# Messages of layers 2 and 3 in two float32r parts, with half of their one-hots made on GpSimd

## The reference

```python
# layer 2
ef = jnp.concatenate([x[row], x[col], edge_attr], axis=-1)
h = ef @ W1 + b1
mu = jnp.mean(h, axis=0); var = jnp.mean((h - mu) ** 2, axis=0)
h = jax.nn.relu((h - mu) * jax.lax.rsqrt(var + BN_EPS) * gamma + beta)
msgs = h @ W2 + b2
sums = jax.ops.segment_sum(msgs, row, num_segments=n_nodes)
counts = jax.ops.segment_sum(jnp.ones((msgs.shape[0],)), row, num_segments=n_nodes)
out = sums / (counts + 1.0)[:, None] + x
# layer 3
m = jax.nn.relu(jnp.concatenate([x[src], et], axis=-1) @ msg_W.T + msg_b)
agg = jax.ops.segment_sum(m, dst, num_segments=x.shape[0])
agg = agg / jnp.clip(deg, 1.0)[:, None]
```

## Time and profile before

| | us |
|---|---|
| median of 3 runs (4504.23 to 4513.55) | 4507.58 |
| the profiled execution's own time | 4506.15 |
| its span in the trace | 4504.0 |
| layer 2, first to last h and adds of a tile | 3037 to 3812 |
| layer 3, first to last h and adds of a tile | 3884 to 4451 |

### The profile page before, as it was taken

One profiled execution on the slowest core, in us unless ns is written; L12 is line 12 of the kernel. 1 busy time (PEld: TensorE's weight loads), 2 busy tenths in 40 slices (PEclk: granted clock), 3 DMA queues, 4 the chain that ended last, 5 costly groups with the idle time before them and its releaser, 6 DMA issues.

```text
span 4504.0 us, 93109 instructions
## 1 busy us (share of the span) xinstructions
PE 3567.1 (79%) x35307; PEld 3108.5 (69%) x35307; DVE 3209.6 (71%) x7198; ACT 2176.5 (48%) x6143; POOL 964.7 (21%) x1005
## 2 busy tenths in 40 slices
PE   1488899889999451666648888669999999699996
PEld 1266666666666331666647887449999998699995
DVE  5589888878898446999868787674444445666666
ACT  2366666667777223788747667212222222333332
POOL 0466577757677400000000000000000000000000
PEclk7799998999999675878779999889999999899998
DMA  5666676767777301000011011333334432233322
GB/s 110 200 186 184 172 205 197 195 171 211 209 214 211 90 5 39 10 12 12 9 35 46 38 45 45 106 109 104 113 109 116 116 109 77 63 102 102 98 97 65
DMA packets 418314, 488.81 MB, mean 109 GB/s; under 512 B 178078, under 2 KB 329924, under 8 KB 417725
## 3 DMA queue, kind: packets, MB, share of 16 engines
q1 hardware_dynamic: 358861, 305.18, 23.7%
q0 software_dynamic: 58992, 177.50, 13.7%
HBM read 376.80 MB, written 105.72 MB: 107 GB/s over the span
## 4 chain that ended last, share of the span: by engine, by line
PE 62%; DVE 22%; ACT 5%; issue 4%; DMA 3%; SPq 2%; POOL 1%; DVEq 0%; POOLq 0%; ACTq 0%
PE bank L3533 6%; PE bank L3496 6%; PE bank L3520 5%; PE bank L3474 5%; PE bank L3476 5%; PE bank L2325 4%; PE bank L2331 3%; PE bank L2336 3%; PE bank L3442 2%; PE bank L2898 2%; PE bank L2316 2%; ACT arena_c L2861 2%; PE bank L2389 2%; PE bank L2307 2%; DVE arena_b L1749 2%
## 5 line engine op out<-in xcount | busy, mean ns | idle before, releaser
L1112 POOL DMA_INDIRECT arena_a<-src_table,src_tix x808 | 775.9, 960 | 353.1 <-issue 228.3
L3279 DVE TENSOR_SCALAR arena_c<-arena_c 128x128 f32<-128x128 f32 x1225 | 268.9, 281 | 402.4 <-PE bank L3496 402.4
L3413 ACT ACTIVATE arena_c<-bank 128x512 f32<-128x512 f32 (+2 forms) x325 | 186.5, 574 | 591.2 <-PE bank L3476 591.2
L2898 PE MATMUL bank<-arena_a,arena_c 128*128 128x150 f32 x1800 | 289.3, 331 | 173.4 <-ACT arena_c L2864 173.4
L3349 DVE TENSOR_SCALAR arena_c<-arena_c 128x128 f32<-128x128 f32 x1225 | 265.7, 280 | 203.6 <-PE bank L3533 203.6
L3474 PE MATMUL bank<-arena_c,arena_a 128*128 128x128 bf16 x3675 | 406.2, 219 | 0.0
L3476 PE MATMUL bank<-arena_c,arena_a 128*128 128x128 bf16 x3675 | 406.2, 219 | 0.0
L2898 PEld LDWEIGHTS bank<-arena_a,arena_c 128*128 128x128 f32 x1800 | 283.7, 225 | 176.5 <-ACT arena_c L2864 176.5
L3428 ACT ACTIVATE arena_c<-bank 128x512 f32<-128x512 f32 (+1 forms) x319 | 185.2, 581 | 386.8 <-PE bank L3520 386.8
L3533 PE MATMUL bank<-arena_c 128*128 128x128 f32 x2450 | 343.1, 282 | 0.0
L3496 PE MATMUL bank<-arena_c 128*128 128x129 f32 x2402 | 338.6, 281 | 0.0
(11 more groups left out here) (583 smaller groups left out, 9263.7 us busy)
## 6 DMA issues: line engine op xcount, KB each, us to landing
y_rows<-arena_c SPq DMA_DIRECT2D x101, 576.0 KB
arena_a<-bucket_rows SPq DMA_DIRECT2D x50, 832.0 KB
arena_a<-bucket_rows SPq DMA_DIRECT2D x50, 768.0 KB
arena_a<-bucket_lists SPq DMA_DIRECT2D x25, 896.0 KB, 4.6
pair_counts<-arena_c SPq DMA_DIRECT2D x25, 800.0 KB
arena_a<-bucket_lists SPq DMA_DIRECT2D x25, 704.0 KB, 4.4
arena_a<-src_table,src_tix POOLq DMA_INDIRECT x808
arena_c<-edge_attr SPq DMA_DIRECT2D x100, 128.0 KB
```

The lines of the kernel that those rows point to most:

```text
L1112: e.indirect_dma_start(out_, None, table, bass.IndirectOffsetOnAxis(ap=idx, axis=0)).then_inc(sem, 16)
L2898: put = e.matmul(bank[2 + s][:, 0:3 * KT], hot_pos[s][:, j, :], routed_v[s][:, j, :, :].rearrange("p f k -> p (f k)"), start=(j == 0), sto ...
L3279: hot = e.tensor_scalar(col_hot[at % 2][:, i, :], iota_row, src_lo[:, b, 2 * k + j:2 * k + j + 1], None, ALU.is_equal)
```

## The change

Both layers get the same edit. A message is kept as two numbers of the type float32r, a float32 of which 12 bits of the significand are kept: ScalarE's rectified message, rounded (part 0), and what the rounding left, rounded (part 1), which VectorE computes from the bank and part 0 in one instruction per group (`dve_low_parts`). The one-hots are float32r too. The adds of a tile are two float32r products of 128 columns, one per part, in place of one f32 product.

The one-hots of the first two tiles of a group stay on VectorE; those of the third and fourth go to GpSimd (`pool_b2_main`, `pool_b3`). The buffers become rings of three (`RING_M`). TensorE does the adds of group n-2 behind h of group n. A bank is free for h of group n+4 when part 1 of group n has been made, not when ScalarE has read it. The column of ones is gone; layer 2's counts come from sums that layer 1 made already (`node_sums`). The unit tests keep their place behind the one-hots of the same group. The core of the diff (the edits for layer 3 on ScalarE and TensorE are like those for layer 2):

```diff
+        RING_M = 3
+        msg_parts = part_buffers("msg_parts", base_b, 0, RING_M, [P, 2, 4, D])
+        msg_parts3 = part_buffers("msg_parts3", base_c, 7304, RING_M, [P, 2, 4, D])
+        node_hot = part_buffers("node_hot", base_a, 10752, RING_M, [P, 4, P])
...
+        def pool_b2_main(e):
+            e.wait_ge(sig.split_dve, 6)
+            for at, (u, k, bs) in enumerate(main_groups()):
+                nt = len(pair_tiles(bs))
+                if nt > 2:
+                    if at >= RING_M:
+                        e.wait_ge(sig.added_pe, at - RING_M + 1)
+                    for i in range(2, nt):
+                        hot = source_hot(e, at, i)
+                    hot.then_inc(sig.col_hot_pool, 1)
+
+        def dve_low_parts(e, at, nt, high_made, low_made, parts):
+            e.wait_ge(high_made, at + 1)
+            to = parts[at % RING_M]
+            e.scalar_tensor_tensor(out=to[:, 1, 0:nt, :], in0=bank[at % 4][:, 0:nt * P].rearrange("p (t f) -> p t f", f=P), scalar=0.0,
+                                   in1=to[:, 0, 0:nt, :], op0=ALU.max, op1=ALU.subtract).then_inc(low_made, 1)
...
                     for i, ts in enumerate(unit3_tiles(u)):
-                        if at >= 2:
-                            e.wait_ge(sig.added3_pe, at - 1)
-                        for i_, t in enumerate(ts):
-                            hot = e.tensor_scalar(col_hot[at % 2][:, i_, :], iota_row, dst_lo[:, b, t:t + 1], None, ALU.is_equal)
+                        dve_low_parts(e, at, len(ts), sig.relu3, sig.low3, msg_parts3)
+                        if at >= RING_M:
+                            e.wait_ge(sig.added3_pe, at - RING_M + 1)
+                        for i_, t in enumerate(ts[0:2]):
+                            hot = target_hot(e, at, i_, b, t)
                         hot.then_inc(sig.col_hot3, 1)
                         at += 1
                         if i == UNIT3_GROUPS[u] - 2 and u + 1 < 2 * NB:
                             dve_unit_hot3(e, u + 1)
...
-                e.activation(msgs[at % 2][:, 0:nt, 0:D], bank[at % 4][:, 0:nt * P].rearrange("p (t f) -> p t f", f=P), ACT.Relu).then_inc(sig.relu, 1)
+                e.activation(msg_parts[at % RING_M][:, 0, 0:nt, :], bank[at % 4][:, 0:nt * P].rearrange("p (t f) -> p t f", f=P), ACT.Relu).then_inc(sig.relu, 1)
...
                     if n >= 4:
-                        e.wait_ge(sig.relu, n - 3)
+                        e.wait_ge(sig.low, NB + n - 3)
...
-                if n >= 1:
-                    at = n - 1
+                if n >= 2:
+                    at = n - 2
...
                     for i in into_k:
-                        put = e.matmul(bank[6 + k % 2][:, 0:D + 1], col_hot[at % 2][:, i, :], msgs[at % 2][:, i, :],
-                                       start=(first and i == into_k[0]), stop=(last and i == into_k[-1]))
+                        for part in range(2):
+                            put = e.matmul(bank[6 + k % 2][:, 0:D], hots[:, i, :], parts[:, part, i, :],
+                                           start=(first and i == into_k[0] and part == 0), stop=(last and i == into_k[-1] and part == 1))
                     put.then_inc(sig.added_pe, 1)
```

More of the change, by code:

```diff
@@ L8 @@
 F32 = mybir.dt.float32
+F32R = mybir.dt.float32r
 I32 = mybir.dt.int32
@@ L3000, in pool_buckets, with target_hot, pool_b3 @@
             e.wait_ge(g.nodes_ready, 4)
+            pool_b2_main(e)
+            pool_b3(e)
+        def target_hot(e, at, i, b, t):
+            return e.tensor_scalar(node_hot[at % RING_M][:, i, :], iota_row, dst_lo[:, b, t:t + 1], None, ALU.is_equal)
+        def pool_b3(e):
+            e.wait_ge(sig.split_dve, 8)
+            at = 0
+            for u in range(2 * NB):
+                for ts in unit3_tiles(u):
+                    if len(ts) > 2:
+                        if at >= RING_M:
+                            e.wait_ge(sig.added3_pe, at - RING_M + 1)
+                        for i in range(2, len(ts)):
+                            hot = target_hot(e, at, i, u // 2, ts[i])
+                        hot.then_inc(sig.col_hot3_pool, 1)
+                    at += 1
         def dve_b_hot(e, b, i):
@@ L3257, in dve_b2_stats @@
             dve_wc_parts(e, own)
-            for s in range(2):
-                e.memset(msgs[s][:, :, D:D + 1], 1.0)
+            own.step(e.tensor_copy(stat[:, 2, :], node_sums[:, 0:NB, 2]))
             dve_split(e, scaled_tables, 2)
@@ L3267, in main_groups, with source_hot @@
             return [(u, u // 2, bs) for u in range(2 * NB) for bs in unit_pairs(u % 2)]
+        def source_hot(e, at, i):
+            u, k, bs = main_groups()[at]
+            b, j = pair_tiles(bs)[i]
+            return e.tensor_scalar(node_hot[at % RING_M][:, i, :], iota_row, src_lo[:, b, 2 * k + j:2 * k + j + 1], None, ALU.is_equal)
+        def pool_b2_main(e):
[13 more added lines that the diff above has]
+                                   in1=to[:, 0, 0:nt, :], op0=ALU.max, op1=ALU.subtract).then_inc(low_made, 1)
         def dve_b2_main(e, own):
             all_groups = main_groups()
-            counts = stat[:, 2, :]
             extras = 0
-            for at in range(GROUPS + 2):
+            for at in range(GROUPS + 3):
                 if at < GROUPS:
                     u, k, bs = all_groups[at]
-                    if at >= 2:
-                        e.wait_ge(sig.added_pe, at - 1)
-                    for i, (b, j) in enumerate(pair_tiles(bs)):
-                        hot = e.tensor_scalar(col_hot[at % 2][:, i, :], iota_row, src_lo[:, b, 2 * k + j:2 * k + j + 1], None, ALU.is_equal)
+                    nt = len(pair_tiles(bs))
+                    dve_low_parts(e, at, nt, sig.relu, sig.low, msg_parts)
+                    if at >= RING_M:
+                        e.wait_ge(sig.added_pe, at - RING_M + 1)
+                    for i in range(min(nt, 2)):
+                        hot = source_hot(e, at, i)
                     hot.then_inc(sig.col_hot, 1)
@@ L3353, in dve_b3 @@
                             dve_unit_hot3(e, u + 1)
[L3354 removed]
+                        if i == 3 and u % 2 == 0 and u:
                             dve_b3_block(e, b - 1)
@@ L3456, in pe_b2_main @@
             e.wait_ge(sig.d_wc, 192)
-            for n in range(GROUPS + 1):
+            by_pool = 0
+            for n in range(GROUPS + 2):
                 if n < GROUPS:
@@ L3504, in pe_b3 @@
             flat = [(u, i, ts) for u in range(2 * NB) for i, ts in enumerate(unit3_tiles(u))]
-            for n in range(len(flat) + 1):
+            by_pool = 0
+            for n in range(len(flat) + 2):
                 if n < len(flat):
@@ L3532, in pe_b3 @@
                     for i_ in range(len(ts)):
-                        put = e.matmul(bank[6 + b % 2][:, 0:D], col_hot[at % 2][:, i_, :], msgs[at % 2][:, i_, 0:D],
-                                       start=(first and i_ == 0), stop=(last and i_ == len(ts) - 1))
+                        for part in range(2):
+                            put = e.matmul(bank[6 + b % 2][:, 0:D], node_hot[at % RING_M][:, i_, :], msg_parts3[at % RING_M][:, part, i_, :],
+                                           start=(first and i_ == 0 and part == 0), stop=(last and i_ == len(ts) - 1 and part == 1))
                     put.then_inc(sig.added3_pe, 1)
```

62 lines of the change are left out of this document (38 added, 24 removed).

## The result

The changed kernel takes 4678.3 us (median of 4 runs, 4675.0 to 4687.6), against 4509.8 us for the kernel before in the same session: a ratio of 1.0382, 95% interval 1.0365 to 1.0399. It is slower, as forecast and inside the range, but by 169 us where the sum said 103. The profiled execution has a span of 4685.8 us, 182 longer than the one of before; it is the longest of the four. The ratios in this document are those on record; the quotient of two medians differs from them by up to 0.0013.

A forecast was written before the change was run, and what follows sets the result against it. TensorE's stream was taken as the bound in layers 2 and 3, the f32 weight load setting the products' pace; -35 + 78 + 29 + 10 + 20 + 1 = +103 on 4506 gave 4610 us, range 4535 to 4700.

The forecast's parts named there:

- The products: Adds on TensorE: load pace stays 0.111 us, the last pass ends sooner, 0.95 becomes 0.89; -35 us, bounds -35 and 0.
- Part 1 ahead of the unit tests: VectorE's queue: tests come late, TensorE waits 2.06 and 1.21 us at layer 3 boundaries (+78), 1.2 in layer 2 (+29).
- GpSimd and VectorE: GpSimd's one-hots and VectorE hold each other up where both run; +10 us taken, bounds nothing and 42 us.
- the 0.5 that was named: Sign to look for in the profile: GpSimd's one-hots under 0.5 us each.
- The rule of the Trainium skill: Shared port pair: VectorE instructions in a two-port mode and GpSimd ones exclude each other; sum then nearer the upper bound.
- The clock: Layer 3: waits might lower TensorE's granted clock, with layer 1's 7% loss as upper case; +20 us, between 0 and 45.
- A clock that falls for long after a wait: Sign that the prediction is wrong: TensorE's clock falling for long after each wait.
- The rest: One more part 1 at each layer's end, +1 us; removed copies, memsets and 49 small additions hidden under TensorE's stream.
- the fast product: Rival, TensorE's adds: float32r product at the bf16 pace of 0.055 us, kernel at 4413 us; chance 0.09.
- the costly one: Rival, TensorE's adds: a rounded product costs a whole f32 product, 0.223 us, kernel about 5010 us; chance 0.06.
- GpSimd as the bound of layer 3: Rival: at 1.1 us per GpSimd one-hot, layer 3's groups take 2.25 us, kernel at 4670 us; chance 0.04.
- the tests were late: Contradicts the rival that unit tests are never late and only shorter adds count, 4471 us; chance 0.02.

The follow-up runs named there:

- e3: e2 plus unit tests one group earlier in layer 2's odd units, and in layer 3 one (even units) or two (odd units) groups earlier; 4499.6 us, ratio 0.9972.
- e2: The changed kernel with VectorE's work on finished blocks, including the extras' addition, ahead of part 1 and the one-hots in layer 2; 4634.9 us, ratio 1.0285.
- e1: The changed kernel with the unit tests of layer 3's odd units two groups earlier; 4587.8 us, ratio 1.0171.
- e4: e3 with both parts side by side in one product of 256 columns per tile, VectorE adding the two halves of a block's sum; 4325.2 us, ratio 0.9588.

## Why the prediction was right, and where its sum was off

The mechanism was right: products at the load's pace win little, and part 1 ahead of the unit tests makes TensorE wait. By its steps:

- *The products* (-35): the sign was right, the size too large. The adds of a four-tile group went from 0.95 to 0.93, not 0.89, and h ahead of them about 0.01 less; the loops of e3 show about -24. The prediction had charged the last pass's saving in full.
- *Part 1 ahead of the unit tests* (+78 in layer 3, +29 in layer 2): the waits were to be 2.06 and 1.21, and are 1.83 and 1.09, so 24 x 2.92 = 70 us. In layer 2 the view's idle time is 19.5, 24 times 0.8; the view counts from the modelled end of the last product, and at the layer 3 boundaries it shows 0.16 less than start to start (1.67 for 1.83), so about 24 x 0.97 = 23. Even units of layer 2 don't wait, as said. A good part of the 0.2 that the waits fall short is adds that take 0.93, not 0.89, and so cover more.
- *GpSimd and VectorE* (+10): 2.5 us as far as the tests are longer, and these are inside the 70 above. GpSimd's one-hot took 0.6 us, twice its row and over the 0.5 that was named, and was still never late for TensorE in layer 3: it is done at least 1.4 us before the weight loads of its adds begin. The rule of the Trainium skill that was weighed there (SBUF — State Buffer, "Who interferes with whom") fits the trace in part: GpSimd's two one-hots take 2.70 us where the tests run and 1.23 elsewhere. But the sum did not come near the upper bound of this term, since it is GpSimd that stands still, off the path.
- *The clock* (+20, bound 45): this term was 38 us too small, and its bound too low. Even units of layer 3 lost 58 us to it (45 in e2's profile, with the same layer 3), and e1, which leaves every even unit's code as it is, gives these 58 back. The average of layer 1 was the wrong row to borrow from; the falls come after 14 of 23 odd waits, and cost the even unit 1.6 to 8.6 us each. A clock that falls for long after a wait was one of the prediction's own signs of being wrong, and for this term it was.
- *The rest* (+1, small additions hidden under TensorE's stream): **this is the step that failed.** The 49 small operations that it weighs, 24 additions and 25 copies for the counts, are those that the change takes away. The extras' 24 additions to the sums stay; they moved one group later and behind part 1 on VectorE's queue, and have no term in the sum. In the last block, where most groups hold two extras, TensorE waits for them; the prediction did not follow who waits for what stands behind part 1 there. It was 33 us in layer 2 (its first to last h grew by 44.1, of which 11 is in the regular units) and 7 more up to layer 3's start; e2 gives 36 of these back.

With the measured sizes: -24 + 70 + 23 + 58 + 40 = 167, against 182 between the two profiles. The part ahead of layer 2 is 12 us longer in this profile (layer 2 starts at 3049.5, before at 3037.4, in the other profiles between 3029.7 and 3045.8), which leaves 3. Layer 2 was to be some 15 us longer and is 44; layer 3 some 90, and is 117.

That the time still lies inside the range is in part luck. The extras had no term and the clock went beyond its bound; the room that the range kept above the sum for GpSimd (32 us) and for products that win nothing (30) was not needed there and took them in.

The rivals: the fast product is excluded by 0.111 between loads, the costly one too; GpSimd as the bound of layer 3 is excluded at 0.6 us a one-hot, below its 1.1, though its 4670 us is by chance the named time that comes closest; and the tests were late.

## What to carry to other kernels

When a step is put ahead of others on a queue, follow every instruction behind it to the engine that waits for it, also in the last iteration, where the mix of work is another: here the small additions that only the last block needs cost 40 us, where the waits that were foreseen cost 93. Where loading the stationary operand sets the pace of the products, fewer loads with wider moving operands pay, and two float32r products in place of one f32 product don't: the same columns in one product turned e3's 0.997 into 0.959. A wait on TensorE that comes again and again is priced with the clock that may follow it, from a run that shows both; the length of the wait alone did not tell which it would be.

## What was not expected of the hardware

- A wait of 1.83 us in each block of layer 3 was followed, in 14 of 23, by several us at the 1.2 GHz level, with TensorE busy all through (granted clock 0.51 in the row of e1's section): in the changed kernel the even unit after the wait takes 13.3 us undisturbed and up to 21.9. A wait of 1.09 us in each block, without those, left the granted clock at 1.00 (e1), and waits of 1.5 us on average left it at 1.00 in e4's stretch too.
- A 128x128 one-hot on GpSimd takes 0.6 us, against 0.28 on VectorE, and about twice as long where VectorE's bf16 tests run (2.70 us for two, against 1.23).
- A float32r product with 256 columns has its load 0.117 us behind the last one ((0.54 - 0.19) / 3), one with 128 columns 0.111: twice the columns for 0.006 us.
